# Low halves of a weight's parts, shared between VectorE and GpSimd in a two-layer LoRA kernel

## The reference

```python
x = x + (einsum('bsd,od->bso', x, W0) + b0 + (x @ A0[id0]) @ B0[id0])
x = x + (einsum('bti,oi->bto', x, W1) + b1 + 2 * (x @ A1[id1]) @ B1[id1])
```

## Time and profile before

| | |
|---|---|
| median of 3 runs | 2088.76 us (2087.1 to 2090.78) |
| profiled execution | 2087.02 us, span 2085.3 us |
| busy share: PE, DVE, ACT, POOL | 99%, 76%, 35%, 35% |
| product 0 and its preparation | about the first 164 us of the span |
| mean granted clock of TensorE | 0.997 of full speed |

### The profile page before, as it was taken

The page is one execution under the profiler, slowest core; times in us unless marked ns, Lnnn a source line. Parts: engine busy times, 40 slices in busy tenths (PEclk is TensorE's granted clock), DMA queues, the critical chain, the costliest instruction groups (busy, mean ns, idle before and its releaser), DMA issues.

```text
span 2085.3 us, 27915 instructions
## 1 busy us (share of the span) xinstructions
PE 2055.9 (99%) x9388; PEld 1708.0 (82%) x9388; DVE 1594.2 (76%) x2177; ACT 724.6 (35%) x1291; POOL 721.3 (35%) x513
## 2 busy tenths in 40 slices
PE   6999999999999999999999999999999999999999
PEld 5887888888888888888888888888888888888887
DVE  6588879977778787677877677877677886777885
ACT  5562323333323333333333333333333333333332
POOL 2135415451404552222444131444040545131453
PEclk9999999999999999999999999999999999999999
DMA  9985747995737796746797665798574789464776
GB/s 291 285 312 172 253 140 234 276 323 159 239 103 235 240 321 179 209 132 195 231 308 231 178 179 153 223 299 273 148 216 134 211 262 332 145 215 121 218 219 194
DMA packets 283898, 458.03 MB, mean 220 GB/s; under 512 B 27500, under 2 KB 88940, under 8 KB 283244
## 3 DMA queue, kind: packets, MB, share of 16 engines
q1 hardware_dynamic: 215788, 333.54, 51.8%
q10 hardware_dynamic: 67968, 122.71, 19.4%
HBM read 382.75 MB, written 74.45 MB: 219 GB/s over the span
## 4 chain that ended last, share of the span: by engine, by line
PE 86%; DVE 5%; DMA 2%; issue 1%; ACT 0%; SPq 0%; POOL 0%; ACTq 0%; DVEq 0%; POOLq 0%
PE acc L1549 27%; PE acc L1555 27%; PE acc L1560 27%; PE h_acc L1477 2%; PE h_acc L1473 2%; PE acc L1487 1%; DVE w_lo L1074 1%; DVE c_acc L1182 1%; DVE x_sum L1089 1%; DMA b_half<-b0t_t 1%; PE h_acc L1476 1%; DVE xop_lo L1100 0%; DVE vp_lo L1069 0%; DVE c_pre L1252 0%; DMA w_raw<-v_t 0%
## 5 line engine op out<-in xcount | busy, mean ns | idle before, releaser
L884 POOL TENSOR_TENSOR w_raw<-w_raw,w_second 128x512 f32<-128x512 f32 x464 | 657.8, 1419 | 1225.7 <-DMA w_second<-wc_t 649.3
L1074 DVE TENSOR_TENSOR w_lo<-w_raw,w_hi 128x512 fp32r<-128x512 f32 x672 | 585.8, 874 | 406.1 <-ACT w_hi L921 404.3
L921 ACT ACTIVATE w_hi<-w_raw 128x512 fp32r<-128x512 f32 x672 | 424.2, 632 | 1230.9 <-PE acc L1560 1046.3
L1549 PE MATMUL acc<-xop_hi,w_hi 128*128 128x512 f32 x2688 | 726.3, 391 | 5.0 <-DVE c_pre L1252 3.1
L1555 PE MATMUL acc<-xop_lo,w_hi 128*128 128x512 f32 x2688 | 722.5, 390 | 0.0
L1560 PE MATMUL acc<-xop_hi,w_lo 128*128 128x512 f32 x2688 | 722.0, 390 | 0.0
L1549 PEld LDWEIGHTS acc<-xop_hi,w_hi 128*128 128x128 f32 x2688 | 502.7, 188 | 110.2 <-issue 4.6
L1560 PEld LDWEIGHTS acc<-xop_hi,w_lo 128*128 128x128 f32 x2688 | 503.6, 188 | 104.1
L1555 PEld LDWEIGHTS acc<-xop_lo,w_hi 128*128 128x128 f32 x2688 | 503.5, 188 | 103.4
L1100 DVE TENSOR_TENSOR xop_lo<-x_sum,xop_hi 128x512 fp32r<-128x512 f32 x240 | 158.5, 680 | 3.8 <-ACT xop_hi L934 3.0
L1252 DVE TENSOR_TENSOR c_out<-acc,c_out 128x512 f32<-128x512 f32 x224 | 149.6, 679 | 4.4 <-PE acc L1487 3.8
(11 more groups left out here) (104 smaller groups left out, 1024.3 us busy)
## 6 DMA issues: line engine op xcount, KB each, us to landing
w_raw<-wc_t SPq DMA_DIRECT2D x448, 256.0 KB, 3.8
w_second<-wc_t ACTq DMA_DIRECT2D x320, 256.0 KB, 4.4
w_raw<-v_t SPq DMA_DIRECT2D x208, 256.0 KB, 4.2
w_second<-v_t ACTq DMA_DIRECT2D x144, 256.0 KB, 4.7
x_in<-x_t SPq DMA_DIRECT2D x128, 256.0 KB, 5.8
out_t<-c_out SPq DMA_DIRECT2D x128, 256.0 KB, 5.4
w_part<-w_t SPq DMA_DIRECT2D x32, 512.0 KB, 8.7
x_pre<-w_t SPq DMA_DIRECT2D x64, 256.0 KB, 6.4
```

The source lines that it names most:

```text
L884: nc.gpsimd.tensor_tensor(w_raw[:, r, :], w_raw[:, r, :], w_second[:, n % RAW2, :], ALU.add if sign > 0 else ALU.subtract).then_inc(w_summ ...
L921: nc.scalar.activation(flat(w_hi[:, s % RING, :, :]), w_raw[:, r, :], ACT.Copy).then_inc(w_hi_ready, 1)
L1074: nc.vector.tensor_tensor(flat(w_lo[:, s % RING, :, :]), w_raw[:, s % RAW, :], f(flat(w_hi[:, s % RING, :, :])), ALU.subtract).then_inc(w_ ...
L1549: nc.tensor.matmul(bank[:, :], w_hi[:, s % RING, kk, :], xop_hi[:, place, :], start=(k == 0), stop=False)
```

## The change

VectorE keeps `vp_lo` of the 16 even parts, and GpSimd makes that of the 16 odd ones. `vp_lo_ready` becomes two semaphores, one for the even and one for the odd parts. In GpSimd's queue the sums are no longer issued one behind the other: the odd part of `parts_split(g)` comes behind sum g + 2. The whole change to GpSimd and VectorE:

```diff
-            for s in range(STEPS):
+            def sum_w(s):
                 (n0, n1), mm = sum_parts(s), s % 2
...
+            def split_part_lo(n):
+                pool.wait_ge(vp_hi_ready, n + 1)
+                nc.gpsimd.tensor_tensor(flat(vp_lo[:, n % 2, :, :]), flat(v_part[:, n % PRAW, :, :]),
+                                        f(flat(vp_hi[:, n % 2, :, :])), ALU.subtract).then_inc(vp_lo_ready[1], 1)
+
+            for s in range(2):
+                sum_w(s)
+            split_part_lo(1)
+            for g in range(STEPS + 1):
+                if g + 2 < STEPS:
+                    sum_w(g + 2)
+                for n in parts_split(g):
+                    if n % 2:
+                        split_part_lo(n)
...
@@ VectorE
-            for n in PARTS_AT[-1]:
-                split_part_lo(n)
+            split_part_lo(0)
...
                 for n in parts_split(g):
-                    split_part_lo(n)
+                    if n % 2 == 0:
+                        split_part_lo(n)
```

More of the change, by code:

```diff
@@ L356, in two_layer_lora_kernel @@
         vp_hi_ready = sem("vp_hi_ready")
-        vp_lo_ready = sem("vp_lo_ready")
+        vp_lo_ready = [sem("vp_lo_even_ready"), sem("vp_lo_odd_ready")]
         gp_done = sem("gp_done")
@@ L433, in b_home, with wait_vp_lo @@
             return b_raw[:, n, :] if n < 2 else b_more[:, n - 2, :]
+        def wait_vp_lo(eng, n):
+            eng.wait_ge(vp_lo_ready[n % 2], n // 2 + 1)
         def stores(b, pl):
@@ L893, in copy_part @@
                     act_e.wait_ge(part_stored[n % PRAW], n // PRAW * 16)
-                    act_e.wait_ge(vp_lo_ready, n - PRAW + 1)
+                    wait_vp_lo(act_e, n - PRAW)
                     if pair < 4:
@@ L1069, in split_part_lo @@
                 nc.vector.tensor_tensor(flat(vp_lo[:, n % 2, :, :]), flat(v_part[:, n % PRAW, :, :]),
-                                        f(flat(vp_hi[:, n % 2, :, :])), ALU.subtract).then_inc(vp_lo_ready, 1)
+                                        f(flat(vp_hi[:, n % 2, :, :])), ALU.subtract).then_inc(vp_lo_ready[0], 1)
             def w_split_lo(s):
@@ L1419, in add_part_g @@
                 pair, mg, _ = PARTS[n]
-                pe.wait_ge(vp_lo_ready, n + 1)
+                wait_vp_lo(pe, n)
                 if n == 0:
```

## The result

The changed kernel takes 2120.41 us (median of 5 runs, 2119.9 to 2123.87) against 2088.76: 1.0156 times, with a 95% interval of 1.0144 to 1.0168. It is slower by 31.7 us. The forecast had the direction and the waits for the copies right, but said 2107.4 and at most 2115.

The account below looks back on a forecast made before the run. TensorE, busy 2055.9 of 2085.3 us, was taken as the bound. Terms 14.3 + 1.0 - 2.4 + 2.4 + 3.3 = +18.6 gave 2105.6, forecast as 2107.4 against the 2088.76 median; range 2095 to 2115, own case 2099 to 2113.

Parts of the forecast that it names:

- The copies (+14.3): Steps 4, 8, 12: ScalarE's copies wait for sums queued behind GpSimd's low halves, stalling TensorE's transposes; 14.3 us, between 10.3 and 15.
- TensorE's pauses: Whole kernel: each new wait of TensorE was priced at its own length, with no term for a lower clock.
- case of knock-on effects: Rival, 2114.8 us, chance 0.12: TensorE's pauses of 4 to 6 us push further work at b0t_lo, M3 and sums 8, 13.
- No later stage has idle time to absorb a shift: Premise for the whole kernel: TensorE is busy 2055.9 of 2085.3 us, so each new wait is paid in full.
- `b0t_lo` (+1.0): Step 3: a 1.14 us low half ahead of it goes, GpSimd's part 7 holds VectorE 2.18; +1.0 us.
- Waits on `vp_lo` (-2.4): Four short TensorE waits before small matmuls on vp_lo vanish, as VectorE has one half less to do; -2.4 us.
- part 30 (+2.4): Wait before part 30: GpSimd's part 31 keeps w_lo out 2.18, part 29's low half takes 0.2; +2.4 us.
- Residual adds in M3 (+3.3): GpSimd's adds run about 9 us late; three meet VectorE's two-SBUF-input instructions before the eviction at 200.65; +3.3 us.
- GpSimd's 1024 columns (2.34): A moved low half on GpSimd takes 2.34 us, bounded by 2.18 and 2.49, and keeps VectorE out for 2.18.
- short holds: Rival, 2094.7 us, chance 0.14: stalls of steps 4, 8, 12 stay at 10.3; VectorE's relief wins the vp_lo waits.
- faster: Rival, 2084 us, chance 0.05: a lighter VectorE removes TensorE's five waits on vp_lo, 5.0 us, and nothing is added.

Follow-up runs that it names:

- The runs with part 7: Changed kernel with each pair of sums issued ahead of the low half: all 16 odd parts on GpSimd 2094.72 us, only part 7 on GpSimd 2092.51.
- the two runs with later adds: Changed kernel, no low half on GpSimd, first residual adds wait for the last part's product: 2089.85 us; also parts 30 and 31 earlier on VectorE: 2089.88.
- parts 9, 17 and 25 alone: Changed kernel with only these low halves on GpSimd: 2107.38 us with them ahead of sums 7, 11 and 15, 2089.35 with the sums ahead.
- the run with later adds: Changed kernel, no low half on GpSimd, pairs of sums issued early, eight first residual adds wait for the last part's product: 2089.85 us.
- parts 30 and 31 first: Changed kernel, no low half on GpSimd, late residual adds, VectorE makes low halves of parts 30 and 31 ahead of w_lo and evictions: 2089.88 us.
- only part 31: Changed kernel with only part 31's low half on GpSimd, pairs of sums issued ahead of it, residual adds behind it: 2090.15 us.
- part 31 in two instructions: Changed kernel with only part 31's low half on GpSimd, made by two instructions of 512 columns, pairs of sums issued ahead: 2089.92 us.
- sums first and all 16 parts: Changed kernel, all 16 odd low halves on GpSimd, each pair of sums issued ahead of the low half once its parts are copied: 2094.72 us.
- without part 7: Changed kernel, all odd low halves except part 7's on GpSimd, each pair of sums issued ahead of the low half: 2089.72 us.

## Why the prediction was wrong

Step by step, in the order of the forecast:

- **The copies (+14.3).** Right in mechanism, place and size: 14.6 in the trace, in steps 4, 8 and 12, and nothing when only the order of the sums is put back. The single pauses were 5.4, 4.6 and 4.6, for 6.0, 4.4 and 3.9, so that the total is better than its parts. In step 4 the turns were not those that I had laid out: `a_lo` held nothing up, and `b_lo` came ahead of the low half and not ahead of the sum.
- **"TensorE's pauses" as a cost only while they last.** This is the step that failed. I priced each standstill at its own length. At and behind four pauses TensorE's granted clock was at 1.2 GHz, for 4.9 to 5.8 us of work each, and for 13.6 us behind `b0t_lo`. These five stretches cost 15.0 us, and the forecast had no term for them; its case of knock-on effects had other causes. The range ended 5 us short for want of it. That 18.6 + 15.0 comes near the 33.2 of the trace is partly luck: part 30 cost more than forecast and the adds in M3 less. The row was at hand. TensorE's longest pause in the kernel before, 8.56 us for W0's first loads, ends at 17.67, and around it the clock stood at half:

```profile
12.20:22.40 10.20, 4.62 (x18) 3.78 (x19) 8.91 (x11) 8.83 (x13) 0.00 (x0) 0.50 1.10 278
```

The rows that I read, and the earlier trace rows, show pauses of 2.2 us at most and a full clock, and I took that to hold for pauses of 4 to 6 us.
- **"No later stage has idle time to absorb a shift"** (ahead of the terms). Not quite: the wait at M3's eviction shrank by 1.6, and the waits behind 260 us by 0.9.
- **`b0t_lo` (+1.0).** Right in size, 0.8 to 1.8. What hung on it was missed: the products behind it are thin, 130 columns, and the clock fell in this execution and in others, 6.5 us here. The runs with part 7 show it in part of the executions. Why the clock falls in some and not in others is open; I tried no run for it.
- **Waits on `vp_lo` (-2.4) and part 30 (+2.4).** The four short ones are gone, as forecast. That before part 30 grew by 3.8, from 2.2 to 6.0, and not by 2.4: the hold of w_lo was right (2.83 here, so 2.15), and the residual add that now follows part 31 holds part 30's low half for another 1.1 (2.30 instead of 1.22), which I had left out.
- **Residual adds in M3 (+3.3).** Wrong: the wait at the eviction in question did not grow, it fell from 2.02 to 0.46. VectorE came to that eviction 32.4 later than before (231.58 for 199.22), and TensorE, slowed behind part 30, came 33.9 later. So some of the slow stretch vanished in this wait. The adds end about 5 us late against TensorE and not 9, because the eight first ones ran in 12.26 us with VectorE idle for part of it; GpSimd was done 7.6 us ahead of the matmul in question. The 2.7 in the row of waits is for the most part another one, 2.26 at 257.29 in M2, where TensorE did not wait before (222.54). VectorE's two `xop_lo` there took 3.48 beside GpSimd's sums, for 2.38; that this is the cause was not tested. A wait of the kind forecast exists, as the two runs with later adds show (4.3 and 7.4 us instead of 2.0).
- **GpSimd's 1024 columns (2.34).** Undisturbed they took 2.38 to 2.44, so my upper bound of 2.49 held; with VectorE's turns in them the 16 have a mean of 2.74 and reach 4.13. The 2.25 that I had worked out from the figure of the Trainium skill (GPSIMD Engine Reference, "Elementwise — side-by-side cycle accounting") was low.

The rival "short holds" (2094.7) is met by no run of the change; "faster" fell with the first trace, for the reason given against it: the copy has no room for 3.6 us.

## What to carry to other kernels

Before work is put into an idle engine's queue, look at who waits for what stands behind it: here 25.7 of 31.7 us went when the sums that others waited for were issued first, and with parts 9, 17 and 25 alone 18.0 went (2107.38 to 2089.35). Price a pause of TensorE at its length plus the slow stretch behind it, in this kernel 2.2 to 2.5 us behind pauses of 4.3 to 6.2 us. And an instruction moved from VectorE to GpSimd still takes VectorE's time wherever two SBUF inputs meet it, 2.17 for 1.14 here, so it should go where VectorE is idle or reads PSUM; VectorE's busy time did not fall with 16 instructions fewer.

## What the runs showed of the hardware that I had not expected

Past the first loads, the granted clock fell to 1.2 GHz at each of TensorE's pauses of 4.3 to 6.2 us, 16 in nine traces, and 22 matmuls in such a pause kept it at 2.4, in step 4 and in step 8. At shorter waits it went either way. After 1.8 us ahead of the thin products of `b0t_lo` it fell in two of three traces. After 2.2 us before part 30 it stayed up in six of seven and fell, briefly, in the run with later adds. At waits for evictions it fell after 3.6 us (parts 30 and 31 first) and after 2.5 us (only part 31), and stayed up after 2.8 and 2.4 us (part 31 in two instructions).

The executions of each version with ten or more of them spread over 5 to 9 us, which is more than most edits of this kind are worth. The clock goes with part of that: with sums first and all 16 parts, the executions at 0.998 and those at 0.992 or 0.993 are 4.4 us apart in the mean. It is not all of it: without part 7, the fastest and the slowest, 2086.6 and 2093.6, both have 0.998.
